# A kernel of eight fused layers on one core: GpSimd raises the variance to its power before the longer memory fills instead of after them, and the two interleaved batches are merged in another order

## The reference, cut to what matters

```python
def _layernorm(x, axis=-1, eps=1e-05):
    m = jnp.mean(x, axis=axis, keepdims=True)
    v = jnp.var(x, axis=axis, keepdims=True)
    return (x - m) / jnp.sqrt(v + eps)

    x = x + _L0_attn_ref(_layernorm(x, axis=-1), ...)
    x = x + _L0_ffn_ref(_layernorm(x, axis=-1), ...)
    x = x + _L1_attn_ref(_layernorm(x, axis=-1), ...)
    ...
    x = x + _L3_attn_ref(_layernorm(x, axis=-1), ...)
    x = x + _L3_ffn_ref(_layernorm(x, axis=-1), ...)
```

## Time and profile before

| | |
|---|---|
| three runs | 1911.11, 1920.31, 1921.92 us (median 1920.31) |
| profiled execution | 1911.35 us, span 1909.3 us, mean granted TensorE clock 0.935 |
| PE busy | 1602.4 us, 84% |
| DVE busy | 1267.7 us, 66% |
| ACT busy | 1025.7 us, 54% |
| POOL busy | 791.0 us, 41% |

### The profile page before, as it was taken

One profiled execution on the slowest core, in us unless ns is written; L12 is line 12 of the kernel. 1 busy time (PEld: TensorE's weight loads), 2 busy tenths in 40 slices (PEclk: granted clock), 3 DMA queues, 4 the chain that ended last, 5 costly groups with the idle time before them and its releaser, 6 DMA issues.

```text
span 1909.3 us, 29013 instructions
## 1 busy us (share of the span) xinstructions
PE 1602.4 (84%) x10660; PEld 920.5 (48%) x10660; DVE 1267.7 (66%) x2849; ACT 1025.7 (54%) x1967; POOL 791.0 (41%) x734
## 2 busy tenths in 40 slices
PE   6789899867988898987787889996778898999867
PEld 3456664313545676521354567651235456754214
DVE  4655558998554464799865455589975545549995
ACT  4555446655555444665455544466545554455654
POOL 2331215885132112588614220268841422117791
PEclk9999999888999998988899999998789999999789
DMA  6004402020000440212000053021100014302110
GB/s 220 1 1 137 133 16 73 28 89 12 12 1 1 141 134 11 73 40 78 12 12 1 4 162 113 14 71 59 55 12 6 1 40 135 111 18 77 49 46 12
DMA packets 91982, 105.41 MB, mean 55 GB/s; under 512 B 7104, under 2 KB 70336, under 8 KB 91584
## 3 DMA queue, kind: packets, MB, share of 16 engines
q1 hardware_dynamic: 89792, 99.37, 16.9%
q0 software_dynamic: 2048, 4.20, 0.7%
HBM read 80.60 MB, written 22.94 MB: 54 GB/s over the span
## 4 chain that ended last, share of the span: by engine, by line
PE 58%; DVE 20%; ACT 11%; POOL 6%; issue 4%; DMA 1%; DVEq 0%; SPq 0%; ACTq 0%; POOLq 0%
PE P L238 12%; DVE M L2038 7%; PE P L1652 6%; PE P L1881 4%; POOL M L2108 3%; PE P L1233 2%; PE P L406 2%; PE P L978 2%; PE P L2166 2%; DVE st L185 2%; PE P L1238 2%; PE P L1249 2%; DVE M L200 1%; PE P L1660 1%; PE P L1205 1%
## 5 line engine op out<-in xcount | busy, mean ns | idle before, releaser
L2038 DVE TENSOR_TENSOR_SCAN M<-P,M 128x512 f32<-128x512 f32 x384 | 444.9, 1204 | 19.5 <-ACT P L1973 17.8
L1973 ACT ACTIVATE P<-M,negA 128x512 f32<-128x512 f32 x384 | 262.3, 689 | 170.5 <-DVE M L2038 167.9
L1881 PE MATMUL P<-M,wt 32*32 32x512 f32 x3072 | 247.0, 712 | 105.4 <-DVE M L2038 64.3
L238 PEld LDWEIGHTS P<-wt,M 128*128 128x128 f32 x2176 | 278.2, 194 | 100.5 <-issue 43.9
L238 PE MATMUL P<-wt,M 128*128 128x128 f32 x2176 | 292.1, 280 | 10.0 <-ACT M L1980 4.0
L2108 POOL TENSOR_TENSOR M<-M 128x512 f32<-128x512 f32 x192 | 238.6, 1273 | 104.6 <-ACT M L1955 75.0
L2108 POOL TENSOR_TENSOR M<-W,M 128x512 f32<-128x512 f32 x192 | 242.9, 1294 | 62.9 <-PE P L1881 62.8
L1881 PEld LDWEIGHTS P<-M,wt 32*32 32x32 f32 x3072 | 38.9, 111 | 251.1 <-DVE M L2038 156.0
L1749 DVE TENSOR_TENSOR M<-M,P 128x512 f32<-128x512 f32 x128 | 87.0, 682 | 76.7 <-PE P L1660 72.5
L1652 PE MATMUL P<-M,wt 128*128 128x512 f32 x256 | 134.5, 607 | 0.8 <-ACT M L1701 0.5
L1701 ACT ACTIVATE M<-P 128x512 f32<-128x512 f32 x128 | 76.4, 597 | 101.2 <-PE P L1652 92.9
(11 more groups left out here) (352 smaller groups left out, 3225.9 us busy)
## 6 DMA issues: line engine op xcount, KB each, us to landing
W<-in_e SPq DMA_DIRECT2D x88, 192.0 KB, 2.7
M<-in_e SPq DMA_DIRECT2D x64, 192.0 KB, 2.6
M<-dt SPq DMA_DIRECT2D x48, 256.0 KB, 4.4
M<-xs SPq DMA_DIRECT2D x32, 256.0 KB, 3.2
ys<-M SPq DMA_DIRECT2D x32, 256.0 KB, 2.3
W<-du SPq DMA_DIRECT2D x32, 256.0 KB, 4.8
W<-xh SPq DMA_DIRECT2D x16, 256.0 KB
M<-du SPq DMA_DIRECT2D x16, 256.0 KB, 4.2
```

The source lines that it names most:

```text
L238: m = e.matmul(out[:, tok(j)], h[:, tok(j)], wgt, start=first and j == 0, stop=last, skip_group_check=True)
L1881: m = e.matmul(t["sums"][i // 2][to:to + 32, :], part("WC", c)[r, r], scan[r, :], start=c == 0, stop=c == 5, tile_position=(32 * i, to))
L1973: e.activation(t["aa"][n % 2][:, :], t["dtr"][i][:, :], EXP, scale=negA[:, c:c + 1]).then_inc(ACT.s, ACT.mark(b, "a3", "aa", n))
L2038: e.tensor_tensor_scan(bb[:, :], t["aa"][n % 2][:, :], bb[:, :], 0.0, MUL, ADD).then_inc(DVE.s, DVE.mark(b, "a3", "scan", n))
```

## The change

In a0 and in a1, the two GpSimd steps of the norm move forward: in a0 ahead of the mask column L597 (both longer fills still stand before them), in a1 directly behind the first fill and so ahead of the fills L1162, L1163 and L1166. Four of the five tables of turns are new (SyncE's stays), with one more turn for each block on GpSimd. Lines of the changed kernel behind the edit in a1 carry a number that is one higher, and the two fills in a1 read L1164 and L1165.

```diff
             e.memset(L.R[10].bitcast(f32), 1.0).then_inc(POOL.s, POOL.mark(b, "a0", "pad"))
             e.memset(L.M[:, 2 * T:4 * T], 0.0).then_inc(POOL.s, POOL.mark(b, "a0", "zeros"))
+            yield from pool_norm(e, w, b, "a0")
             yield
             w.wait_ge(POOL.s, POOL.of(b, "a0", "zeros"))
             w.wait_ge(w_in[0], 16)
             own = wv("own").unsqueeze(1).to_broadcast([128, 16, 4])
             e.tensor_tensor(va[:, :, :, :, 8].rearrange("p k g h -> p (k g) h"), own, own, MUL).then_inc(
                 POOL.s, POOL.mark(b, "a0", "ones"))
-            yield from pool_norm(e, w, b, "a0")
...
             e.memset(L.M[:, T:3 * T], 0.0).then_inc(POOL.s, POOL.mark(b, "a1", "zeros"))
+            yield from pool_norm(e, w, b, "a1")
+            yield
             e.memset(L.M[:, 17 * T:17 * T + 256], 0.0)
             e.memset(L.MR[:, 11 * T:15 * T].bitcast(f32), 1.0)
             yield
             w.wait_ge(POOL.s, POOL.of(b, "a1", "zeros"))
             e.memset(L.M[:, T:3 * T].rearrange("p (a n) -> p a n", n=32)[:, :, 8:18:9], 1.0).then_inc(
                 POOL.s, POOL.mark(b, "a1", "ones"))
-            yield from pool_norm(e, w, b, "a1")
...
-            "gpsimd": (682,
-                "01fc1c1fc0de0e0e0000000702400fffffffcffd7f0cff003ff031e38e00000004c90003fffffefbfcffc33fc1c1fc0de0e3"
+            "gpsimd": (690,
+                "01fc1c0ff03783b80000002a300003fffe7fffffff303f18d0ff031e3f000000001284803ffff3fffff5fc33f19c0ff03783"
```

More of the change, by code:

```diff
@@ L2266, in program @@
             "tensor": (2211,
[L2267 to L2270, removed]
@@ L2271, in program @@
-                "0b584c95ff07b201b33e800366436ffc2d77fffe07f0800001089840ef0c70ffe237bb3ccd140f7fe10fe1be136e80000000"
-                "3cf003e1ed519feeeeeefdddee87a576ac12bffffff08f8506dfe"),
-            "scalar": (1644,
[L2274 to L2278, removed]
@@ L2279, in program @@
-            "vector": (2247,
[L2280 to L2285, removed]
@@ L2286, in program @@
-            "gpsimd": (682,
-                "01fc1c1fc0de0e0e0000000702400fffffffcffd7f0cff003ff031e38e00000004c90003fffffefbfcffc33fc1c1fc0de0e3"
-                "40000002320400fffffff6ff5ff0cff0707f037838b00000004c90003fffffffffffccc"),
+                "00000211028836dff826fffff50fe1000000224321ee18e1ffc46f76799a281eff843f15e19aec404000003cf007df85b649"
+                "fbdddddfbf76174ad70225e95ffd7f0c90fc200780d9440800ee09effffff77d2f8b400000112190ef271a3ffcc36e30c334"
+                "97ff017c1f0f3de72000001e780d481fe0b649fddddddffc78c1e92c6c0fe8b5fc2615ff03d01010f107e400f707f7dbffff"
@@ new lines, in program @@
+                "f547f0400000112190f70dfdff9c7e2e6d2870863bfe01e0f0f3dd000001b1e06a403df0dae49fbbbbbbff743c92d54017c2"
+                "eb09867fff03750079bd80038855bfc365fffffa87e1400000112190f70c70ffe237638430c6ffe187d1df0f3de620040000"
+                "0007bcda7b28f7bbbbbf777777c1e93bc03d7ffffff08f8a1e67e"),
+            "scalar": (1644,
+                "003000333318e7ff69dd800412405b66faf6dec889740b369ad480afceb582040a4924aa022109b7d915feffbedbfffff820"
+                "f043cc1a005b233ff7db6dd80082480b766fd7b238d13e0496e773409fa6de20810292492c80010489a6fff7fff76bfffdda"
+                "5848b04133f017a707ffbf2dd600209202dbf3fbebf24119602cb73b404bf33ea8108092492580848254fb913f7fed6ff769"
+                "697fe85c7fe0080dae06fbfed36d80082480b6cdf5d9888d6f60536e7728809f6d045141292495249041112b7f3fffbfffff"
+                "fffe8d888ff"),
@@ new lines, in program @@
+            "vector": (2247,
+                "0000180ffa98501de00000051b7e006f3ffdbdf976c90180000488c3d57f3ffffb02c346036014a017eae6d7e023ffa89924"
+                "924a65f4a80022a81e7ababff7fffffab40df81037ec2003fb7201f0bbf800000364fc5f3ffedefcf6c90180001424403f3f"
+                "ff683b7f2c30178505c07f2f3cfe402bfea2a492490c030be950004b5ffaaaffaadffe07bff8007707800fffeda80efcbd40"
+                "00001e7f407cfffebdf3db240603840100fcfe43ebffff01a0180d850a05fa79e7f224babe46492492a97d2a00022a807d55"
+                "7fdd5a077ffd5ff300fc1ede603ffe7580efe00000029b7e01f3fff6f7cf6c90180000488900fffa03f7f2fe8f0278505900"
+                "bf42034fff15ff324924924952fa540005e3fefffffffffff986aa01ffe07e"),
@@ L2289, in program @@
+            "gpsimd": (690,
+                "01fc1c0ff03783b80000002a300003fffe7fffffff303f18d0ff031e3f000000001284803ffff3fffff5fc33f19c0ff03783"
+                "f0000000a8900003fff7effcffffc33fc1c0ff019e38380000001309003fffffffffffccc"),
             "sync": (191,
```

## The result

The changed kernel took 1951.97, 1945.84, 1938.68 and 1937.62 us (median 1942.26), against 1917.83 for the kernel before beside it. The ratio is 1.0137, 95% interval 1.0084 to 1.0191: slower by 26 us, where -7.6 was forecast and the range ended at 1930. A later set of runs gave 1.0116 (1.0088 to 1.0144).

A forecast was written before the change was run, and what follows sets the result against it. It took DVE as the bound while two blocks scan, and dependent steps of two lanes at handovers. Norm steps -3.6 and order -4.0 gave -7.6 us, from the mean 1916.2 to 1909 us; range 1892 to 1930.

The forecast's parts named there:

- The order term, -4.0: New merging order: half of each lane's shift counts; first handover +5.5, second 0, third -6, last pair -3.5; net -4.0 us.
- put at +5.5: First handover: block 2 starts 12 to 20 us later, blocks 1 and 3 are 5 us earlier; half counted, +5.5 us.
- put at -9.5: Third handover -6 us, with blocks 6 and 7 earlier, and last pair -3.5 us, with block 6 reaching its scans earlier.
- The slower rival: After the first handover block 2's late start passes to its scans and everything behind: +16, 1932 us; chance 0.17.
- The faster rival (-28): Odd lane alone sets the handovers, block 2's delay is hidden, all earlier starts count: -28, 1888 us; chance 0.38.
- The norm steps, -3.6: Moved GpSimd norm steps in a1: block 2 -1.7, block 4 -1.3, block 0 -1.3, block 1's L746 +0.7; sum -3.6 us.
- block 4 -1.2 (put at -1.3): a1 of block 4: L200's 2.77 us wait for GpSimd's power shrinks, gaining 1.3 us.
- block 2 -1.7 in the old order (put at -1.7): a1 of block 2: the power comes 1.7 us earlier; bounds -2.7 to +1.3, since block 3's steps may queue ahead.
- block 0's L287 -1.4 (-1.3): a1 of block 0: DVE's L287, no longer beside GpSimd's long fill, falls from 1.76 to 0.45 us: -1.3 us.
- L746 +0.9 (+0.7): Small DVE step of block 1, now beside block 0's moved fill: a loss of 0.7 us.
- The odd blocks, put at 0: a1 of blocks 1, 3, 5, 7: L200 stays behind the even block's divisions, so an earlier power gains 0.
- Block 6, also put at 0: Block 6: power earlier and L200 moved forward, but the chain passes on other work; 0, at best -2.8 us.

The follow-up runs named there:

- first handover: New order only from the middle of the first pair's scans to block 3's a0, norm steps moved, against the kernel before: 1928.3 us, ratio 1.0039.
- behind it to the second handover: New order only from block 3's a0 to block 4's a0, norm steps moved, against the kernel before: 1930.0 us, ratio 1.0060.
- the middle piece: New order only from block 4's a0 to the middle of the third pair's scans, norm steps moved, against the kernel before: 1932.7 us, ratio 1.0068.
- last stretch: New order only from the middle of the third pair's scans to the end, norm steps moved, against the kernel before: 1914.3 us, ratio 0.9972.
- the first two: New order from the middle of the first pair's scans to block 4's a0, norm steps moved, against the kernel before: 1936.9 us, ratio 1.0086.
- norm only: Norm steps moved, old order of merging kept, against the kernel before: 1917.2 us, ratio 0.9990.
- fillers: 14 unused PE transposes in idle spells ahead of three clock falls, added to the middle piece: 1927.9 us, ratio 1.0036 to the kernel before.
- the best kernel: The kernel of the last stretch, against the kernel before: 1914.3 us, ratio 0.9972.
- extra work elsewhere: 14 unused PE transposes at places without a clock fall, added to the middle piece: 1935.6 us, ratio 1.0079 to the kernel before.
- 59 fillers on the best kernel: 59 unused PE transposes ahead of L200 waits at 11 places, added to the best kernel: 1922.8 us, ratio 1.0015 to the kernel before.

## Why the prediction was wrong

**The order term, -4.0: this is the step that failed.** It let half of each lane's shift count, as if the order acted through lanes that are early or late. Measured on top of the norm steps: first handover +9 to +11 (put at +5.5), behind it to the second handover +13 (put at 0), the middle from block 4's a0 on +15 (not priced), last stretch -3.5 (put at -9.5). These add up to 34 us and the whole order cost 24, so a piece's cost alone is not its share in the whole; the first two make +18 together and not 23. What the runs showed in place of the shifts is a term the sum didn't have, PE's time at half clock: the middle piece and the first handover have no more idle time of PE than norm only and 62 to 65 us more at half clock, and fillers took some 6 us of the middle's 15 back. Behind the first handover idle time grew too, by 8 us, and what of that piece's 13 us is clock is open.

**The slower rival named another mechanism.** It wanted block 2 late after the first handover. With that handover alone, block 2's first scan starts at 793.4 for 780.8 in norm only; 2.4 us of it were there before the handover. These are the two stretches of that kernel, first scans and second front:

```profile
312.40:460.70 148.30, 114.48 (x1002) 41.47 (x1008) 140.20 (x164) 89.99 (x146) 123.14 (x102) 0.90 0.17 52
460.70:793.40 332.70, 293.30 (x1660) 192.59 (x1668) 170.35 (x545) 168.44 (x349) 74.59 (x81) 0.93 0.16 47
```

and of norm only:

```profile
310.00:464.50 154.50, 122.95 (x1014) 45.68 (x1020) 144.42 (x173) 94.75 (x157) 124.70 (x104) 0.86 0.17 51
464.50:780.80 316.30, 276.38 (x1651) 184.10 (x1657) 167.85 (x536) 163.08 (x339) 72.15 (x80) 0.96 0.17 50
```

PE's idle time in the front is 39.4 for 39.9 us, its clock 0.93 for 0.96. The start is late since PE is slow, and since 6 us of scans became work behind them; PE did not wait longer in the front, as it would if block 0's late f3 had held it up. The sign was that rival's, the reason was not. The faster rival (-28) is out with the first two pieces.

**The bounds.** The prediction named the clock and the middle parts (a2, f2) as what could make it wrong, and gave neither a price, nor a place in the range. The sum took the clock of the earlier trace rows as given. Yet the profile before showed falls of the clock behind idle spells in the fronts; that the new order spreads these spells anew was to be asked. A small slip beside it: the window in the earlier trace rows ends at 1404.00 and not at 1404.4; 1404.4 is where block 5's last scan ends in the trace.

**The norm steps, -3.6.** Their priced terms held: block 4 -1.2 (put at -1.3), block 2 -1.7 in the old order (put at -1.7) and 0.9 in the new, where block 3's steps stand in between, block 0's L287 -1.4 (-1.3), L746 +0.9 (+0.7), and no loss of L200 beside the fills. Norm only gives -2 us (ratio 0.9974 to 1.0006), which agrees with -3.6 and with nothing.

**The odd blocks, put at 0: wrong in the new order.** I wrote that the new order leaves their L200 behind the divisions of the even block. It doesn't. L200 of block 5's a1 in norm only, and then in the changed kernel, each with the last statistics ahead of it:

```profile
1068.23 0.36 DVE L189 BATCH_NORM_AGGREGATE st<-st 128x2 f32<-128x6 f32 x4
...
1072.09 0.75 DVE L200 TENSOR_TENSOR M<-M,st 128x256 f32<-128x256 f32 x2
```

```profile
1101.50 0.19 DVE L189 BATCH_NORM_AGGREGATE st<-st 128x2 f32<-128x6 f32 x2
...
1103.16 0.76 DVE L200 TENSOR_TENSOR M<-M,st 128x256 f32<-128x256 f32 x2
```

3.5 us from statistics to L200 became 1.5, in all four odd blocks. With the old norm in the new order it is 2.9. Block 6, also put at 0, went from 4.26 us in the kernel before to 1.53. That fits the moved steps being worth some 7 us beside new orders and 2 beside the old one, in sign and rough size. It isn't seen in the stages: of the 5.6 us between the profiled executions of the last stretch with the moved and with the old steps, 5.0 lie in the first front, which differs by 9 us between the two executions of the changed kernel.

**What stays open.** The two profiled executions of the changed kernel have 8 to 9 us more idle time of PE than norm only. In the scans of blocks 2 and 3 PE waits 39.6 us for 31.7, and block 3's first scan starts 8.8 us after block 2's last, where in norm only it starts 2.4 ahead of it; that stage as a whole is 1.8 to 3.9 us longer. What of the waiting reaches the end wasn't separated. Nor do the pieces settle how much of the whole 24 us is clock: over all its runs the changed kernel is granted 0.915 to 0.919 for norm only's 0.924, 21 to 35 us more at half clock, worth up to 10 to 17. Within the runs of one kernel 1 us more at half clock went with about 0.25 us, perhaps since much of it falls where DVE is the bound; at that rate it would be 5 to 9 us. So a good part of the 24 us has no shown cause.

## What to carry to other kernels

Where PE is busy 85% of a stage, hold its busy time against its idle time in the profile after a change of order: where busy grew with the same instructions, look at the granted clock before any wait. Try a new order piece by piece, since its whole hides which piece pays: here three cost 9 to 15 us each and the fourth gained 3. Fillers are no sure cure: in two of three places they held the clock, in the third they stood at the start of the spell and the clock fell all the same, extra work elsewhere gained nothing, and 59 fillers on the best kernel cost 8 us. Where a filler must wait for an early result, look whether the clock has fallen before it starts.

## What the runs showed of the hardware

Two L615 take 1.12 us or 2.04 by the granted clock of the moment, so the fall behind a spell of 1.19 us of idle PE, with others of 0.7 behind it, cost 2.7 us in f0 of block 5. In norm only the same spells in f0 of block 5 (1.19, 0.69 and 0.78 us) were followed by no fall. So these alone don't decide it, and what else does, these runs do not say. The Trainium skill ("SBUF — State Buffer", Who interferes with whom) has it that DVE's tensor_scalar in its two-port mode is held up by any GpSimd instruction, one that only writes too; the trace agrees once more, and from a size that I hadn't expected: L746, 32 columns and 0.17 us, took 1.03 beside the fill.
